# A causal attention block followed by a mixture feed-forward block: the feed-forward prelude of chunks 0 and 1 is placed in the last head's slots

## The reference, cut to what matters

```python
def attention(x):
    q, k, v = split(x @ Wqkv.T)            # per head, positions are added to q and k
    scores = where(causal, q @ k.T / 8, -inf)
    return (softmax(scores) @ v) @ Wo.T    # heads concatenated

def ffn(x):
    xn = layernorm(x, ln_g, ln_b)
    abel = gelu(xn @ aw1 + ab1) @ aw2 + ab2                      # 128 -> 512 -> 128
    w = softmax over the top 2 of (xn @ gate_w + gate_b)         # 6 experts
    h = gelu(xn @ ew1[e] + eb1[e]); eo = h @ ew2[e] + eb2[e]     # 128 -> 256 -> 128 each
    nonabel = sum_e(w[e] * eo)
    for i in range(4): nonabel = nonabel @ expm(gens[i])         # 4 rotations, 128 x 128
    gate = sigmoid(concat(abel, nonabel) @ gc_w + gc_b)
    return x + abel * (1 - gate) + nonabel * gate

y = layernorm(x + attention(x))
out = layernorm(y + ffn(y))
```

## Time and profile before

| | |
|---|---|
| median of three timed runs | 697.62 us (696.67 to 697.83) |
| the profiled execution | 695.79 us, of which 694.1 us from the first to the last instruction |
| busy, share of the span | PE 93%, DVE 71%, ACT 65%, POOL 72% |
| eight heads, one every 57.23 us | 42.5 to 497 us |
| feed-forward prelude | 502.3 to 533.6 us |
| section 0 | 533.6 to 576.4 us |
| sections 1 to 4 | 576.4 to 694.1 us |

### The profile page before, as it was taken

One profiled execution on the slowest core, in us unless ns is written; L12 is line 12 of the kernel. 1 busy time (PEld: TensorE's weight loads), 2 busy tenths in 40 slices (PEclk: granted clock), 3 DMA queues, 4 the chain that ended last, 5 costly groups with the idle time before them and its releaser, 6 DMA issues. The chain is left out here.

```text
span 694.1 us, 10135 instructions
## 1 busy us (share of the span) xinstructions
PE 644.0 (93%) x3215; PEld 491.7 (71%) x3215; DVE 495.8 (71%) x1047; ACT 449.0 (65%) x626; POOL 502.0 (72%) x290
## 2 busy tenths in 40 slices
PE   5979999999999999999999999999797899989883
PEld 4657778777777777777877777776586687667651
DVE  3578668678777866866977887681297878776684
ACT  3547667676776676766767767676456477657561
POOL 8028888898888988888888888899753356567660
PEclk9999999999999999999999999999988899999996
DMA  7532222312222221322132222207000000000001
GB/s 196 137 76 62 47 46 62 77 45 47 47 69 69 47 47 46 83 55 46 46 68 68 47 47 47 47 0 196 3 2 1 0 2 1 1 16 0 15 1 31
DMA packets 29076, 33.75 MB, mean 49 GB/s; under 512 B 6977, under 2 KB 15970, under 8 KB 28898
## 3 DMA queue, kind: packets, MB, share of 16 engines
q1 hardware_dynamic: 29026, 33.14, 19.9%
HBM read 6.84 MB, written 1.05 MB: 11 GB/s over the span
## 5 line engine op out<-in xcount | busy, mean ns | idle before, releaser
L357 POOL TENSOR_TENSOR probs_l<-probs,probs_h 128x1024 fp32r<-128x1024 f32 (+1 forms) x160 | 347.4, 2185 | 96.2 <-ACT probs_h L399 50.5
L454 DVE TENSOR_REDUCE m_part<-max_ps 128x1 f32<-128x512 f32 (+2 forms) x320 | 180.0, 602 | 84.2 <-PE max_ps L529 63.4
L396 ACT ACTIVATE probs<-scores 128x1024 f32<-128x1024 f32 (+1 forms) x160 | 150.5, 941 | 125.8 <-PE scores L558 67.1
L590 PE MATMUL out_ps<-probs_h,v 128*128 128x512 f32 (+5 forms) x640 | 186.1, 374 | 2.1 <-POOL probs_l L357 2.1
L399 ACT ACTIVATE probs_h<-scores 128x1024 fp32r<-128x1024 f32 (+1 forms) x160 | 149.7, 936 | 0.0
L859 POOL TENSOR_TENSOR hid_lo<-hid,hid_hi 128x512 fp32r<-128x512 f32 x64 | 84.0, 1317 | 53.8 <-ACT hid_hi L939 41.4
L557 PE MATMUL scores<-q,k 128*128 128x512 f32 (+1 forms) x320 | 122.0, 382 | 0.0
L590 PE MATMUL out_ps<-probs_l,v 128*128 128x512 f32 (+1 forms) x320 | 116.4, 364 | 0.0
L558 PE MATMUL scores<-q,k 128*128 128x512 f32 (+1 forms) x320 | 116.3, 364 | 0.0
L590 PEld LDWEIGHTS out_ps<-probs_h,v 128*128 128x128 f32 (+1 forms) x640 | 95.7, 163 | 23.9 <-POOL probs_l L357 5.8
L529 PE MATMUL max_ps<-k,q 128*128 128x512 f32 (+2 forms) x320 | 101.8, 393 | 5.6 <-DVE m_part L454 5.2
(11 more groups left out here) (195 smaller groups left out, 977.3 us busy)
## 6 DMA issues: line engine op xcount, KB each, us to landing
k<-qk SPq DMA_DIRECT2D x96, 128.0 KB, 2.3
q<-qk SPq DMA_DIRECT2D x96, 128.0 KB, 2.3
q<-m_turn SPq DMA_DIRECT2D x128, 0.5 KB
v_all<-L_ffn_ew SPq DMA_DIRECT2D x2, 768.0 KB, 7.9
probs<-L_attn_x SPq DMA_DIRECT2D x4, 256.0 KB, 4.3
pos<-positions SPq DMA_DIRECT2D x1, 1024.0 KB, 6.6
out<-v_all SPq DMA_DIRECT2D x4, 256.0 KB, 2.3
acc<-L_attn_Wqkv SPq DMA_DIRECT2D x6, 128.0 KB, 2.9
```

Of the source, the lines that this page charges most:

```text
L357: pool.tensor_tensor(probs_l[:, p % 2, :, lo:CH], probs[:, p % 2, :, lo:CH], probs_h[:, n % 3, :, lo:CH], ALU.subtract).then_inc(S["probs_ ...
L396: act.activation(probs[:, p % 2, :, lo:CH], scores[:, p % 2, :, lo:CH], ACT.Exp, scale=D ** -0.5).then_inc(S["probs_ready"], 1)
L454: dve.tensor_reduce(m_part[:, r, j:j + 1], max_ps[:, u % 2, 0:width], AX.X, ALU.max).then_inc(S["tile_max_ready"], 1)
L590: last = pe.matmul(o_ps(h, c)[0:rows, lo:CH], v, pr, start=(p == PAIR0[c] and j == 0 and k == 0), stop=(p == PAIR0[c + 1] - 1 and j == 1 a ...
```

## The change

Five things are changed.

1. `acc` of chunk 0 is turned on PE in slot 10 of the last head, that of chunk 1 in slot 15, into the free `max_ps`; DVE adds the input and runs both norms of chunk 0 in slots 11 to 16 and of chunk 1 in slots 17 to 21 (50 steps each, in groups of 4 tiles; `half`, `t` and `bits` lie in PSUM, `var` and `guess` in SBUF). PE turns the normed chunk 0 in slot 18, where it waits for those 50 steps; ACT takes it in slot 19. ACT rounds the weights in slots 9, 11, 13, 16 and 23, DVE makes the low part of two of eight weight parts in slots 12 and 17, POOL makes scaled identities in slot 22, ACT scaled generators in slot 24. The loads of the feed-forward arrays are issued in slot 0 of the last head. Tiles are laid over dead ones.
2. The feed-forward prelude is what is left: PE turns the generators and chunks 2 and 3; section 0 begins right behind. The other six low weight parts are made by POOL between the blocks of section 0.
3. All squarings stand in section 0, two steps in each of the blocks 4 to 11. There are 7 in place of 10, with five more Taylor terms in three rounds (`SERIES`).
4. The causal mask of the maxima is added by DVE: a diagonal unit is an addition of 128 columns into `m_diag` and a reduction of the columns left of it (none for the first row tile), and each chunk has one more reduction, of `m_diag` (128 x 512). The product L531 is gone.
5. The projection of chunk 2 moves from slot 10 to 11; the inversions of chunks 1 and 2 move one slot later (`INVERT`).

```diff
-SQUARINGS = 10
+SQUARINGS = 7
-TURN_AT = {1: 5, 3: 6, 5: 7, 7: 8, 9: 9, 11: 10}
-SQUARE_AT = {2: 5, 4: 6, 6: 7, 8: 8, 10: 9}
-PRODUCT_AT = {12: 0, 13: 1, 14: 2}
+STEPS_AT = {0: (1,), 2: (2,), 3: (3,), 4: (4, 5), 5: (6, 7), 6: (8, 9), 7: (10, 11), 8: (12, 13), 9: (14, 15),
+            10: (16, 17), 11: (18, 19), 12: (20,), 13: (21,), 14: (22,)}
+W_LOW_AT = {0: 2, 2: 3, 3: 4, 5: 5, 7: 6, 9: 7}
+ROWS_AT = {10: 0, 15: 1}
+NORM_AT = {11: (0, 8), 12: (0, 9), 13: (0, 9), 14: (0, 8), 15: (0, 9), 16: (0, 7),
+           17: (1, 8), 18: (1, 12), 19: (1, 12), 20: (1, 9), 21: (1, 9)}
+FEATURES_OUT_AT, FEATURES_IN_AT, FEATURES_LOW_AT = 18, 19, 23
+WEIGHT_HIGH_AT = {9: (0,), 11: (1,), 13: (2,), 16: (3,), 23: (4, 5, 6, 7)}
+WEIGHT_LOW_AT = {12: 0, 17: 1}
+GENERATORS_AT, IDENTITIES_AT = 24, 22
-PROJECT = {0: (0, 1), 6: (1, 1), 10: (2, 1), 16: (3, 1)}
+PROJECT = {0: (0, 1), 6: (1, 1), 11: (2, 1), 16: (3, 1)}
+INVERT = {3: (3, -1), 5: (0, 0), 10: (1, 0), 16: (2, 0)}
...
+        def small_sums(c):
+            stats, mean_var, own, pause = early.ln
+            half, t, bits = (max_ps[:, c, n * TPC:(n + 1) * TPC] for n in range(3))
+            return stats, mean_var, (own[:, 0, 0:TPC], half, own[:, 1, 0:TPC], t, bits), pause
...
-                        dve.tensor_reduce(m_part[:, r, j:j + 1], max_ps[:, u % 2, 0:width], AX.X, ALU.max).then_inc(S["tile_max_ready"], 1)
+                        if j < c:
+                            dve.tensor_reduce(m_part[:, r, 2 + j:3 + j], max_ps[:, u % 2, :], AX.X, ALU.max).then_inc(S["tile_max_ready"], 1)
+                        elif r == 0:
+                            dve.tensor_tensor(m_diag[:, r, :], max_ps[:, u % 2, 0:P], mask_qk[:], ALU.add).then_inc(S["tile_max_ready"], 1)
+                        else:
+                            dve.tensor_tensor(m_diag[:, r, :], max_ps[:, u % 2, width - P:width], mask_qk[:], ALU.add)
+                            dve.tensor_reduce(m_part[:, r, 1:2], max_ps[:, u % 2, 0:width - P], AX.X, ALU.max).then_inc(S["tile_max_ready"], 1)
...
+                            dve.tensor_reduce(m_part[:, :, 0], m_diag[:], AX.X, ALU.max).then_inc(S["diagonal_max_ready"], 1)
...
-                if j == c:
-                    last = pe.matmul(max_ps[:, u % 2, width - P:width], mask_kq[:, P:2 * P], ident_b[:], start=False, stop=True)
...
+                    if last == FEATURES_OUT_AT:
+                        pe.wait_ge(S["first_norms_steps"], 2 * ln_steps(TPC))
+                        for t in range(TPC):
+                            turned = pe.transpose(max_ps[:, 0, t * P:(t + 1) * P], early.n2[:, t, :], ident[:])
+                        turned.then_inc(S["features_turned"], 1)
...
+            step(0)
+            for c in range(2, NC):
+                for t in range(TPC):
+                    last = pe.transpose(ps[:, c, t * P:(t + 1) * P], acc[:, (c * TPC + t) * P:(c * TPC + t + 1) * P], ident[:])
+                last.then_inc(S["attention_turned"], 1)
+            pe.wait_ge(S["features_low_ready"], 1)
+            pe.wait_ge(S["features_ready"], 2)
+            section(0, True, False, first=True)
```

More of the change, by code:

```diff
@@ L621, in layer_norm @@
 def layer_norm(dve, sem, base, src, dst, buf, n):
-    stats, mean_var, s, pause = buf
-    var, half, guess, t, bits = (s[:, i, 0:n] for i in range(5))
+    stats, mean_var, (var, half, guess, t, bits), pause = buf
     if not isinstance(base, int) or base > 0:
@@ L748, in feed_forward @@
         logits = sb("logits", [P, NT, NX])
-        before = sb("before", [P, NX, NX])
         gt = sb("gt", [P, NT // 2, NX, NX])
@@ L867, in _ @@
             scale = 2.0 ** -SQUARINGS
-            act.wait_ge(S["early_generators_loaded"], 16)
-            act.activation(gen[:], gens_sb, ACT.Copy, scale=scale).then_inc(S["generator_scaled"], 1)
-            act.activation(series[:], gens_sb, ACT.Copy, scale=scale / 6).then_inc(S["generator_scaled"], 1)
-            for h in range(2):
-                act.wait_ge(S["generator_turned"], h + 1)
-                act.activation(gen_t[:, half(h), :], turn_bank(h), ACT.Copy, scale=scale).then_inc(S["generator_turned_taken"], 1)
@@ L950, in section @@
                             high(c, j - 1)
+                    if first and j == FIRST_FEATURES_AT:
+                        to_features(1)
+                        act.wait_ge(S["loaded_eb2"], 32)
+                        act.activation(eb2_hi[:], eb2_rows[:], ACT.Copy).then_inc(S["eb2_high_ready"], 1)
                     if first and j == FIRST_TANH_AT:
@@ L1080, in weights_low @@
                 dve.tensor_tensor(wt[32:64, cs], ps[32:64, 2 + c if c < 2 else 7, :], wt[32:64, cs], ALU.subtract).then_inc(S["expert_weights_low_ready"], 1)
-            dve.wait_ge(S["early_x_loaded"], 16)
-            residual(0)
-            residual(1)
-            for _ in norms(0):
-                pass
             residual(2)
@@ L1190, in multiply @@
                 return last
-            for h in range(2):
-                turn(gens_sb, h, "generator_turned")
-            for h in range(2):
-                pe.wait_ge(S["generator_scaled"], 1)
-                pe.wait_ge(S["generator_turned_taken"], h + 1)
-                multiply(product(h), gen_t, gen, h)
-                multiply(turn_bank(h), gen, gen_t, h).then_inc(S["generator_squared"], 1)
-            for h in range(2):
-                pe.wait_ge(S["series_steps"], h + 2)
-                for i in range(HALF):
-                    r = HALF * h + i
-                    pe.matmul(product(h)[:, i, :], gen2_t[:, r, :], series[:, r, :], start=True, stop=False)
-                    last = pe.matmul(product(h)[:, i, :], gen_t[:, r, :], ident[:], start=False, stop=True)
-                last.then_inc(S["series_multiplied"], 1)
             def turn_e(k):
@@ L1225, in square, with step @@
                     multiply(product(h), e_turn, e_sum, h).then_inc(S["exponential_squared"], 1)
+            def step(n):
+                if n == 0:
+                    for h in range(2):
+                        turn(gens_sb, h, "generator_turned")
+                elif n == STEP_SQUARE:
+                    for h in range(2):
+                        pe.wait_ge(S["generator_scaled"], 1)
+                        pe.wait_ge(S["generator_turned_taken"], h + 1)
+                        multiply(product(h), gen_t, gen, h)
+                        multiply(turn_bank(h), gen, gen_t, h).then_inc(S["generator_squared"], 1)
+                elif n < STEP_ROUNDS:
+                    k, end = n - STEP_SERIES, n == STEP_ROUNDS - 1
+                    for h in range(2):
+                        pe.wait_ge(S["series_steps"], 2 * k + h + 1)
+                        for i in range(HALF):
+                            r = HALF * h + i
+                            last = pe.matmul(product(h)[:, i, :], gen2_t[:, r, :], series[k][:, r, :], start=True, stop=not end)
+                            if end:
+                                last = pe.matmul(product(h)[:, i, :], gen_t[:, r, :], ident[:], start=False, stop=True)
+                        last.then_inc(S["series_multiplied"], 1)
+                elif n < STEP_PRODUCTS:
+                    k, squaring = divmod(n - STEP_ROUNDS, 2)
+                    if squaring:
+                        square(k)
+                    else:
+                        turn_e(k)
+                else:
+                    k = n - STEP_PRODUCTS
+                    if k == 0:
+                        pe.wait_ge(S["last_exponential_ready"], 1)
+                        pe.wait_ge(S["turned_exponential_taken"], 2 * (SQUARINGS + 1))
+                    else:
+                        pe.wait_ge(S["rotation_taken"], k)
+                    pe.matmul(product(0)[:, 0, :], e_turn[:, NROT - 2 - k, :], rot[:, k - 1, :] if k else e_last[:],
+                              start=True, stop=True).then_inc(S["rotation_multiplied"], 1)
@@ L1284, in layer2 @@
                 for k, (a, h) in enumerate(((w_hi, hid_hi), (w_lo, hid_hi), (w_hi, hid_lo))):
-                    last = pe.matmul(into, a[:, w], h[:, r, :], start=(k == 0 and j in (0, NA)), stop=(end and k == 2 and j < NA))
+                    last = pe.matmul(into, a(w), h[:, r, :], start=(k == 0 and j in (0, NA)), stop=(end and k == 2 and j < NA))
                 last.then_inc(S["second_layer_done"], 1)
@@ L1319, in section @@
                         weights_turned(WEIGHTS_AT[j])
[L1320 to L1333 removed]
+                    if first and j in STEPS_AT:
+                        for n in STEPS_AT[j]:
+                            step(n)
                     if prev and j < LAG:
```

423 lines of the change are left out of this document (257 added, 166 removed).

## The result

| | before | after |
|---|---|---|
| median of four timed runs | 697.73 us (696.67 to 697.84) | 701.51 us (701.06 to 702.56) |
| ratio, 95% interval | | 1.0062 (1.0041 to 1.0083) |
| profiled execution | 695.79 us, span 694.1 | 701.06 us, span 699.3 |
| first scores of head 0 | 42.5 us | 44.3 us |
| a middle head | 57.23 us | 56.7 us |

A forecast was written before the change was run, and what follows sets the result against it. PE's issue was taken to bound seven of eight heads, POOL the last from slot 9; -11.3 + 18.0 + 0.8 - 11.1 = -3.6 us gave 694.0 us on the median's scale, range 679 to 704 (8 in 10).

The forecast's parts named there:

- Part 1: All heads: moving the masks of the maxima from PE to DVE saves 11.3 us.
- +1.9 ahead of head 0: Ahead of head 0, where DVE sets the pace, its new mask work costs 1.9 us.
- so this is covered on average: Middle heads: DVE's 14.2 us idle a head hides its 4.4 us of new mask work.
- a term of 1 us over all heads for the crowded slots: Allowance for DVE being late in crowded slots such as slot 10: 1 us in all.
- Rival 2: Heads: DVE sets every head's pace, PE waits for maxima, the masks gain 0; 705.3 us, chance 0.18.
- Part 2: Last head: norms in its slots wait behind POOL; block ends 18.0 us later, plus 0.8 us.
- the row turns: Last head, slots 9 to 16: PE's two row turns and ACT's weight roundings delay POOL's chain, +0.8 us.
- R: Last head, slot 18: PE restarts once chunk 0's 50 norm steps are done, at 501.3 us in old-trace times.
- the walk through the slots: Last head: chunk 0's norm steps timed in order, applications ending at 493.7, sums at 496.5, then POOL at rest.
- Rival 1: Last head: waits behind POOL don't add up, norms cost only +3 + 0.8 us; 679.0 us, chance 0.17.
- Part 3: Prelude and section 0: 23.0 us less up to block 4, 11.9 more after; -11.1 us.
- Rival 3: Section 0 stalls 1 us more at each pair of steps, +7 us; 701 us, chance 0.12.

The follow-up runs named there:

- masks: Kernel before with only the masks of the maxima moved to DVE and both slot-table moves; 695.94 us, ratio 0.9990 to the kernel before.
- masks_low_later: The run masks with slot 1's low part of the projection made behind that slot's reductions; 689.49 us, ratio 0.9897 to the kernel before.
- after_free_sums: Changed kernel with the last head's small norm sums (variance, guess) in PSUM, applications unchanged; 698.26 us, ratio 1.0012 to the kernel before.
- before_low_later: Kernel before, masks still on PE, with slot 1's low part of the projection behind its reductions; 699.36 us, ratio 1.0010.
- free_low_later: Changed kernel with a PSUM operand in every norm step of the last head and slot 1's low part behind its reductions; 685.74 us, ratio 0.9829.
- after_short_low: Changed kernel with POOL's subtraction cut to 8 columns in slots 11 to 19 of the last head; 690.30 us, ratio 0.9911 to the kernel before.

## Why the prediction was wrong, step by step

**Part 1, the step that failed.** The forecast was -11.3 us. The gain on PE was sized rightly: slot 9, which has two masks, went from 2.78 to 2.54 us. The +1.9 ahead of head 0 was right too (1.8). What failed is the step from DVE's idle 14.2 us a head to "so this is covered on average", with a term of 1 us over all heads for the crowded slots and slot 10 named as one. DVE got less new work than I had (3.6 us a head for 4.4), yet PE lost 1.4 us a head to it, ten times the allowance: measured -0.7 (masks). 0.8 of the 1.4 arise in slots 0 to 2, where a chunk's end, the positions and a low part that waits for ACT follow each other; the rest lies in slots 4, 5, 7 and 15, and slot 10 has none. Rival 2 had the mechanism, PE waiting for reductions, with a chance of 0.18 and passing break-even at 0.5 us of PE waits a head. Its reason, that DVE can't keep two units a slot, is not what slot 2 shows: masks_low_later has the same load and gets 6.4 us back by the order of DVE's queue alone. For the other 0.8 us a head it is not ruled out. So of the 10.6 us that were missing the order of slot 1 explains some 6, and the cause of some 4 stays open. The order could have been read before: the idle time of 0.67 us ahead of L439, behind which slot 1's reductions stand, is in the trace of before, and I took no row of it.

**Part 2.** The forecast was +18.8 with the row turns. From slot 11's start to the second block it was 471.36 to 502.31 before and 470.85 to 518.03 after: +16.2, and 0.8 in slot 10. The mechanism was right in its parts: `var`, the squarings with their PSUM output and the applications waited, the steps that read a tensor from PSUM did not. R was 498.8, or 499.3 in the times of the old trace (slot 11 begins 0.5 us sooner in the changed kernel), against 501.3; from R to the block's end it was 19.2 against 19. So R came 2.0 us earlier, and that is what two errors against each other leave. The four applications of the first norm were to end at 493.7 and ended at 487.9 (488.4 in old times), since the last two ran free (POOL was waiting for ACT from 487.3 to 487.7), and the sums of the second norm began 5.1 us before my 496.5. But POOL was then not at rest, as I had it, and `var` and a squaring of the second norm waited for 3.2 us together. Where the walk through the slots had six waits in the first norm and none in the second, the trace has four and two; that part 2 came so near is in part luck. Rival 1 (the waits don't add up) is out as a forecast, but after_free_sums shows a grain of it: four of the six blocked norm steps give a third of the gain. The Trainium skill, "SBUF — State Buffer", section "Who interferes with whom", says that a VectorE instruction with two SBUF inputs contends with a GpSimd instruction that reads SBUF; the squaring of 1.96 us with its output in PSUM agrees with it.

**Part 3.** The forecast was -11.1, measured 181.3 - 191.8 = -10.5. Block 4 stood at 22.9 us (23.2), blocks 5 to 11 at 4.0 us each, section 1 at 580.7 - 518.0 = 62.7 (63). Blocks 4 to 15 lasted 39.8 us, as worked out (27.9 + 11.9). Up to section 1 that makes -11.4; the remaining +1.0 stands in sections 3 and 4 (54.75 us for 53.76), which were not changed and last from 52.3 to 55.1 us in the profiles of these runs. Rival 3 did not occur.

**Sum.** Measured from the traces: -1.3 up to slot 10 without the row turns, +17.0, -10.5: +5.2 for the profiled executions (+5.3 with what lies around the spans). The forecast was -11.3 + 18.8 - 11.1 = -3.6. Of the 8.8 us between them, part 1 is 10.0 and part 3 0.6, and part 2 gave 1.8 back.

## What to carry to other kernels

An engine's idle share over a loop says nothing about a slot in which several of its steps fall together: before work is moved to it, walk its in-order queue through the fullest slot and see what stands behind a wait for a third engine. Where an engine is late, put a step that waits for another engine behind those whose operands are already there, and leave in front what fills a wait anyway; where it is not late, as in before_low_later, the same move brings nothing. Small VectorE steps beside a busy GpSimd should read one of two tensors from PSUM; here a blocked one cost up to 2.4 us, the rest of the GpSimd instruction under way, and curing four of six gave a third of the gain.

## What the runs showed of the hardware

- A scalar_tensor_tensor of four or 128 columns with one SBUF input and the other from PSUM, also as a broadcast, takes 0.16 and 0.34 us while POOL's subtraction of 2.4 us is under way; a tensor_scalar of 128 columns from SBUF to SBUF then takes up to 2.44 us, and it does so too when its scalar operand lies in PSUM (after_free_sums). Four applications cost DVE 1.11 us as tensor_scalar with POOL at rest (497.65 in the changed kernel) and 1.12 us in the new form with POOL busy (475.45 in free_low_later).
- A tensor_scalar of four columns from SBUF to SBUF waited (1.68 us), one from SBUF to PSUM at 488.81 in free_low_later, with POOL busy from 488.10 to 490.94, took 0.17. So what counts is the form of the step, not its size: a squaring of two SBUF inputs waited with its output in PSUM, a step of one SBUF input did not. The Trainium skill, "SBUF — State Buffer", section "Who interferes with whom", says that a VectorE instruction with at most one SBUF input does not contend with GpSimd unless it is in a 2-port mode, and that tensor_scalar can be in one. The 0.17 and the 1.68 us fit that, though no run here shows the mode itself.
- The mean granted clock was 0.68 from R to the second block in the changed kernel; PE's stop of 6.9 us lies just ahead of that stretch and the one of 7.4 us inside it. It was 0.66 between 495 and 515 us in after_short_low, which has only one such stop, of 7.6 us.
